# Moving a router fold to the layer transition, and another element order in the output copies, in a two-layer attention and mixture-of-experts kernel

## Chip, cores and metric

The kernel runs on one core of a Trainium2 chip. The metric is the device time of one execution in microseconds. The engines work side by side and meet only at semaphores: TensorE (PE in the rows; its weight loads are PEld), VectorE (DVE), ScalarE (ACT), GpSimd (POOL) and SyncE (SP), which here only starts DMAs. Each engine runs its own instructions in the order in which they are written.

## The reference

x has 4 x 24 x 16 tokens of 256 channels (1536 tokens). Twice, with other weights:

```python
x = x + attention(_ln_c(x))                  # 16 heads of 16
t = tokens(x)
t = t + moe(_ln_t(t))                        # 8 experts, top 2

# attention: q and k are means over the 16 pixels, so scores are 24 x 24 per head and batch;
# v keeps the pixels
out = softmax(q k^T / 4) v                   # reshaped back to (B, N, P, C)
y = out @ W_proj + b_proj
# moe, layer 0: softmax(x @ gate_w + gate_b), top 2, silu(x @ w1 + b1) @ w2 + b2, weighted
# moe, layer 1: top 2 of x @ router_w, softmax of the two, (a * silu(g)) @ W2 + b2, weighted
```

Both norms subtract the mean and divide by the deviation, without weights. All is float32.

## The kernel before

One core holds x in `xres`, 12 tiles of 128 tokens. Per layer the stages follow each other: norm, transposes, attention, projection with the residual, second norm and router logits, a table that sorts token and expert pairs into blocks of 128 rows, and a loop of MoE blocks, which takes most of the time. Nobody plans the order: it is written out by hand, one instruction stream per engine.

**The router fold.** The logits of the second norm are linear in x, so the kernel adds E = 8 columns to the attention's products rather than transposing the normalised x again. For that it needs, per layer, (1) the column-centred router weights, kept in columns 3C to 3C+E of `wqkv` (`centre()`, L940, on VectorE, after column sums on TensorE, L1330), (2) `b_route` = centred weights times the projection bias, two small products (L949), (3) the projection weights transposed on TensorE (L1406) and copied to `wprojT` (L1023), (4) their product with the centred weights (L1414) and the sum of `b_route` over channels (L1417), all in bank 5, and (5) two small copies of the results to `wproj` and `b_logit` (L1028, L1030). Semaphore `fold` counts 7 steps per layer, `fold_mm` 3. Before the change both layers do (3) to (5) within the attention: TensorE between `scores(3)` and `attn_transpose(0)`, VectorE between the softmax steps.

**Attention.** TensorE makes values for two pixels at a time (`values(j)`, L1360) in three banks that ScalarE empties (L731), the scores (L1371), the transposes of the probabilities (L1379), attention times values (L1434), then 8 groups of four transposes (L1445). ScalarE (even groups, L789) and VectorE (odd groups, L1046) copy these from PSUM to `outT`; the projection (L1458) waits for all eight. VectorE adds the projection to `xres` (L1073) and takes statistics (L916). Part of the logits goes through DRAM and back (`x_logits`) and is scaled on VectorE (L1063, L1064).

**Weight rounding.** Expert weights are split in a high and a low part. For the first three experts there are 12 pieces: ScalarE rounds a piece (`first_high`, L686), GpSimd subtracts (L611). Both share the time of the attention; `first_high(a, b)` calls stand between ScalarE's other steps. Piece 10 of GpSimd waits until VectorE has done the x_logits sums (`HELD_SPLIT`). All three experts go through one raw buffer, so a piece's DMA waits for an earlier piece's subtraction.

**The transition.** At the end of layer 0's blocks the rows of the last two blocks are not scattered but added on chip: TensorE multiplies them by one-hot rows (`last_rows(j, n)`, L1589) for six pairs of tiles, VectorE adds pair j to `xres` (L963), takes statistics (L916, L922), ScalarE the square root (`deviations`, L696), VectorE the reciprocal and `less_mean` (L933), and the normalised tiles (ScalarE L702, VectorE L937) are transposed (L1344) and copied (L707). VectorE sums pixels from the same banks (`xm`, L988), from which come queries and keys (L1392). `keep_busy` (L1324) are filler products without result.

Of the kernel before, what the change touches and what calls it, by code (L numbers as in the profile page):

```python
# [46 lines left out]
EARLY_PAIRS = (1, 2)  # L47
HELD_SPLIT = 10
# [99 lines left out]
def metaformer(nc, x, conv_w, ffn_w, out):  # L148

    with ExitStack() as ctx:  # L150
# [526 lines left out]
        def _(act):  # L677
# [10 lines left out]
            for L in range(2):  # L688
# [73 lines left out]
                values_out(5)  # L762
                attn_out(0)
                attn_out(1)
                if L == 0:
                    first_high(5, 6)
# [7 lines left out]
                first_high(*((6, 8), (8, 9))[L])  # L774
                for j in range(0, 8, 2):
                    act.wait_ge(s.av_mm, j + 1)
                    if j == 0:
                        act.wait_ge(s.aT_mm, HGROUPS)
                    nc.scalar.copy(o_sb[:, :, 2 * HD * j:2 * HD * (j + 1)].rearrange("p q (h d) -> p h q d", h=2),
                                   bank[j % 4][0:BN, :].rearrange("p (h q d) -> p h q d", h=2, q=PIX)  # L780
                                   ).then_inc(s.o_act, 1)
                    if j < 4:
                        first_high(8 + L + j // 2, 9 + L + j // 2)
# [3 lines left out]
                for j in range(0, 8, 2):  # L787
                    act.wait_ge(s.oT_mm, j + 1)
                    nc.scalar.copy(outT[:, j // 4, :, 4 * (j % 4):4 * (j % 4) + 4].rearrange("p n q -> p q n"),  # L789
                                   bank[4 + j % 4][:, 0:4 * BN].rearrange("p (q n) -> p q n", q=4)).then_inc(s.o_act, 1)  # L790

                first_high(10 + L, 12)
# [102 lines left out]
                if L == 0:  # L895
                    high_pieces(1, 0, PIECES)
                    nc.scalar.activation(table_out[:, 4:5], all_ones[:, 0:1], ACT.Sqrt)


        @block.vector  # L900
        def _(dve):
# [5 lines left out]
            for L in range(2):  # L907
# [32 lines left out]
                def centre():  # L940
                    dve.wait_ge(fold_mm, FOLD_MM * L + 1)
                    dve.wait_ge(s.route_in, 48 if L == 0 else 32)
                    centred = wqkv[:, :, 3 * C:3 * C + E]
                    nc.vector.scalar_tensor_tensor(out=centred, in0=bank[5][:, 0:E].unsqueeze(1).to_broadcast([P, KC, E]),
                                                   scalar=-1.0 / C, in1=wroute[:, :, :], op0=ALU.mult, op1=ALU.add
                                                   ).then_inc(fold, 1)
                    dve.wait_ge(fold, FOLD * L + 1)
                    for k in range(KC):
                        nc.vector.tensor_scalar(b_route[:, k, :], centred[:, k, :], b_col[:, k:k + 1], None, ALU.mult  # L949
                                                ).then_inc(fold, 1)  # L950
# [40 lines left out]

                dve.wait_ge(s.qk_mm, 1)
# [34 lines left out]
                dve.wait_ge(fold_mm, FOLD_MM * L + 3)  # L1027
                nc.vector.tensor_copy(wproj[:, :, C:C + E], bank[5][:, 0:KC * E].rearrange("p (k e) -> p k e", k=KC)  # L1028
                                      ).then_inc(fold, 1)
                nc.vector.tensor_copy(b_logit[:, :], bank[5][:, KC * E:KC * E + E]).then_inc(fold, 1)  # L1030
# [13 lines left out]
                for j in range(1, 8, 2):  # L1044
                    dve.wait_ge(s.oT_mm, j + 1)
                    nc.vector.tensor_copy(outT[:, j // 4, :, 4 * (j % 4):4 * (j % 4) + 4].rearrange("p n q -> p q n"),  # L1046
                                          bank[4 + j % 4][:, 0:4 * BN].rearrange("p (q n) -> p q n", q=4)
                                          ).then_inc(s.o_dve, 1)
# [264 lines left out]
        def _(pe):  # L1313
# [18 lines left out]

            pe.wait_ge(busy_ready, 1)
# [3 lines left out]
            for L in range(2):  # L1337
# [46 lines left out]
                pe.wait_ge(fold, FOLD * L + 1)  # L1384
# [19 lines left out]
                for kd in range(KC):  # L1404
                    for k in range(KC):
                        mm = pe.transpose(bank[5][:, (KC * kd + k) * P:(KC * kd + k + 1) * P],  # L1406
                                          wproj[:, k, kd * P:(kd + 1) * P], ident[:, :])
                mm.then_inc(fold_mm, 1)
                values(4)
                values(5)  # L1410
                pe.wait_ge(fold, FOLD * L + 4)
                for k in range(KC):
                    for kd in range(KC):
                        pe.matmul(bank[5][:, k * E:(k + 1) * E], wprojT[:, kd, k * P:(k + 1) * P],  # L1414
                                  wqkv[:, kd, 3 * C:3 * C + E], start=(kd == 0), stop=(kd == KC - 1))
                for k in range(KC):
                    mm = pe.matmul(bank[5][:, KC * E:KC * E + E], all_ones[:, :], b_route[:, k, :],  # L1417
                                   start=(k == 0), stop=(k == KC - 1))
                mm.then_inc(fold_mm, 1)
# [183 lines left out]
                if L == 0:  # L1603
# [37 lines left out]
```

## Time and profile before

| | |
|---|---|
| three runs, us | 573.47, 575.12, 576.9 (median 575.12) |
| span of the profiled execution | 569.2 us; its own time outside the span is not listed |
| PE busy | 527.7 us, 93% |
| PE weight loads | 468.0 us, 82% |
| VectorE busy | 342.1 us, 60% |
| ScalarE busy | 347.2 us, 61% |
| GpSimd busy | 254.5 us, 45% |
| chain that ended last | PE 70%, VectorE 12%, issue 5%, DMA 4%, ScalarE 4% |
| mean granted TensorE clock | 0.984 |

The span runs from the first to the last instruction of one profiled execution; the runs' times also hold what lies around it. "Busy" is a sum over the whole span and says nothing of a single stage; the chain of waits tells which engine a stage hangs on. Layer 0's attention lies at about 14 to 64 us, its blocks at 83 to 278, the transition at 278 to 300, layer 1's attention to 345, its blocks from 366 on.

### The profile page before, as it was taken

The numbers are of one execution on the slowest core, as the hardware profiler recorded it, in microseconds if no ns is written. First come the engines' busy times: TensorE is split into PE (matmuls) and PEld (weight loads), VectorE is DVE, ScalarE is ACT, GpSimd is POOL, SyncE is SP. The second block draws the span as 40 slices with busy tenths as digits, with TensorE's granted clock in tenths as the row PEclk, the third lists the DMA queues.
The fourth block names the chain that finished last, engine by engine and source line by source line (L and its number), as shares of the span: only waits on it lengthen the run. The fifth ranks groups of instructions, "written<-read, shape, count | busy, mean of one in ns | idle before, by whom it ended". The sixth has DMA issues, their size and how long they took to land.

```text
span 569.2 us, 15318 instructions
## 1 busy us (share of the span) xinstructions
PE 527.7 (93%) x3512; PEld 468.0 (82%) x3513; DVE 342.1 (60%) x791; ACT 347.2 (61%) x676; POOL 254.5 (45%) x278
## 2 busy tenths in 40 slices
PE   7999969999999999999979999699999999999982
PEld 3887538889999999998858874499999999999981
DVE  6448874555533555554794578755677676757441
ACT  6776545666655666666457745555777676676530
POOL 4649033443544455553515360424444455545422
PEclk9999989999999999999989999899999999999997
DMA  8636825876432543226432238354365555212110
GB/s 277 184 108 154 291 89 145 270 183 175 119 56 39 144 120 83 35 37 178 134 132 86 69 108 268 117 196 116 98 180 133 138 150 160 47 35 41 32 19 10
DMA packets 49037, 70.54 MB, mean 124 GB/s; under 512 B 9182, under 2 KB 40560, under 8 KB 49008
## 3 DMA queue, kind: packets, MB, share of 16 engines
q1 hardware_dynamic: 35216, 56.41, 31.4%
q0 software_dynamic: 10464, 13.58, 13.4%
q10 hardware_dynamic: 3328, 0.20, 0.4%
q8 instruction: 14, 0.23, 0.2%
q14 instruction: 15, 0.12, 0.1%
HBM read 57.55 MB, written 13.47 MB: 125 GB/s over the span
## 4 chain that ended last, share of the span: by engine, by line
PE 70%; DVE 12%; issue 5%; DMA 4%; ACT 4%; DVEq 2%; ACTq 1%; POOLq 0%; POOL 0%
PE banks L1316 16%; PE banks L1318 16%; PE banks L1317 16%; PE banks L1532 6%; PE banks L1360 5%; PE banks L1434 2%; DVE stats L916 2%; PE banks L1497 2%; PE banks L1371 1%; DMA mid_dram<-region_b,scol 1%; ACT onehot_blk L812 1%; DMA expert_io<-xn_dram,gcol 1%; PE banks L1324 1%; DVEq L1197 1%; DVE xres L1073 1%
## 5 line engine op out<-in xcount | busy, mean ns | idle before, releaser
L1316 PE MATMUL banks<-w_hi,xT_hi 128*128 x336 | 119.3, 355 | 4.0 <-DVE xT_lo L1188 2.6
L1318 PE MATMUL banks<-w_hi,xT_lo 128*128 x336 | 114.9, 342 | 0.0
L1317 PE MATMUL banks<-w_lo,xT_hi 128*128 x336 | 114.3, 340 | 0.0
L1316 PE MATMUL banks<-w_hi,hT_hi 128*128 x364 | 107.9, 296 | 3.8 <-DVE hT_lo L1263 3.8
L1317 PE MATMUL banks<-w_lo,hT_hi 128*128 x364 | 102.8, 282 | 0.0
L1318 PE MATMUL banks<-w_hi,hT_lo 128*128 x364 | 102.8, 282 | 0.0
L638 POOL DMA_INDIRECT mid_dram<-region_b,scol x26 | 50.7, 1948 | 74.8 <-DMA mid_dram<-region_b,scol 22.3
L611 POOL TENSOR_TENSOR w_lo<-raw,w_hi 128x1024 fp32r<-128x1024 f32 (+2 forms) x24 | 58.9, 2468 | 52.9 <-ACT w_hi L686 42.3
L836 ACT COPY banks<-seed_rows 128x672 f32 (+1 forms) x84 | 69.0, 822 | 19.8 <-DVE h_sb L1280 10.0
L638 POOL DMA_INDIRECT out_dram<-region_b,scol x26 | 45.7, 1757 | 72.1 <-DVE region_b L1298 19.7
L1316 PEld LDWEIGHTS banks<-w_hi,hT_hi 128*128 128x128 f32 x364 | 69.3, 190 | 7.2 <-issue 6.3
L627 POOL DMA_INDIRECT expert_io<-xn_dram,gcol x52 | 53.0, 1020 | 41.5 <-POOL gcol L623 41.5
L1263 DVE TENSOR_TENSOR hT_lo<-banks,hT_hi 128x512 fp32r<-128x512 f32 (+1 forms) x112 | 63.5, 587 | 12.2 <-issue 5.4
L857 ACT CAST hT_hi<-banks 128x512 fp32r<-128x512 f32 (+1 forms) x112 | 55.2, 535 | 25.4 <-PE banks L1532 24.2
L1316 PEld LDWEIGHTS banks<-w_hi,xT_hi 128*128 128x128 f32 x336 | 63.2, 188 | 8.3 <-issue 4.9
L870 ACT ACTIVATE h_sb<-banks 128x512 f32<-128x512 f32 x56 | 33.5, 599 | 59.0 <-PE banks L1318 57.2
L1317 PEld LDWEIGHTS banks<-w_lo,hT_hi 128*128 128x128 f32 x364 | 69.5, 191 | 0.0
L1318 PEld LDWEIGHTS banks<-w_hi,hT_lo 128*128 128x128 f32 x364 | 69.4, 191 | 0.0
L1318 PEld LDWEIGHTS banks<-w_hi,xT_lo 128*128 128x128 f32 x336 | 63.0, 188 | 4.7
L1317 PEld LDWEIGHTS banks<-w_lo,xT_hi 128*128 128x128 f32 x336 | 63.4, 189 | 3.4
L1197 DVE TENSOR_TENSOR w_lo<-raw,w_hi x40 | 48.4, 1209 | 16.5 <-issue 15.7
L1532 PE MATMUL banks<-ident,h_sb 128*128 128x128 f32 (+1 forms) x392 | 52.0, 272 | 0.0
(206 smaller groups left out, 898.2 us busy)
## 6 DMA issues: line engine op xcount, KB each, us to landing
raw<-in_L_ffn_w_dram SPq DMA_DIRECT2D x32, 512.0 KB, 4.0
raw<-in_L_ffn_W_dram SPq DMA_DIRECT2D x16, 672.0 KB, 4.0
seed_rows<-in_L_ffn_b_dram SPq DMA_DIRECT2D x8, 672.0 KB, 4.5
seed_rows<-in_L_ffn_b_dram SPq DMA_DIRECT2D x8, 512.0 KB, 3.9
xn_dram<-raw SPq DMA_DIRECT2D x6, 512.0 KB, 3.2
raw<-in_L_ffn_W_dram SPq DMA_DIRECT2D x8, 384.0 KB, 3.4
raw<-in_L_ffn_W_dram SPq DMA_DIRECT2D x8, 256.0 KB
wqkv<-in_L_conv_W_qkv_dram SPq DMA_DIRECT2D x2, 768.0 KB, 5.8
```

What stands on the lines that cost most here:

```text
L611: pool.tensor_tensor(w_lo[:, e, at], raw[:, 0, at], w_hi[:, e, at].bitcast(F32), ALU.subtract).then_inc(s.pool_split, 1)
L627: pool.indirect_dma_start(out=xg[:, half * C:(half + 1) * C], out_offset=None, in_=xn_dram, in_offset=bass.IndirectOffsetOnAxis(ap=rows, a ...
L638: pool.indirect_dma_start(out=acc, out_offset=bass.IndirectOffsetOnAxis(ap=scol[:, n:n + 1], axis=0), in_=rows, in_offset=None, bounds_che ...
L836: nc.scalar.copy(banks[:, chunks, 0:f.chunk], seed_row(L, e % SEED_ROWS)[:, 0:f.wide] .rearrange("p (c n) -> p c n", c=f.chunks)[:, chunks ...
L857: nc.scalar.copy(hT_hi[:, part, :], bank[4 + j][:, 0:(part.stop - part.start) * P] .rearrange("p (k s) -> p k s", s=P)).then_inc(s.hT_hi, 1)
L870: nc.scalar.activation(h_sb[:, f.chunk * j:f.chunk * (j + 1)], bank[j][:, 0:f.chunk], ACT.Silu).then_inc(s.h, 1)
L1197: less = nc.vector.tensor_tensor(low, raw[rows, (q // PIECES) % 2, at], w_hi[rows, slot, at].bitcast(F32), ALU.subtract)
L1263: nc.vector.tensor_tensor(hT_lo[:, part, :], bank[4 + j][:, 0:(part.stop - part.start) * P] .rearrange("p (k s) -> p k s", s=P), hT_hi[:, ...
L1316: pe.matmul(out, hi, w_high, start=first, stop=False, skip_group_check=onto)
L1317: pe.matmul(out, hi, w_low, start=False, stop=False, skip_group_check=onto)
L1318: return pe.matmul(out, lo, w_high, start=False, stop=last, skip_group_check=onto)
L1532: mm = pe.transpose(bank[4 + j][0:rows, o:o + P], tile, ident[:, :])
```

## The change

Layer 1's steps (2) to (5) move to the transition. TensorE does them between `last_rows` of pairs 1 and 2 (transposes) and of pairs 3 and 4 (products); ScalarE, behind its last rounding of layer 0, does the `b_route` scalings and the copies that VectorE did. Layer 0 keeps its fold in the attention; its `b_route` products move on VectorE behind the xm sums. The copies to `outT` go through the same elements in another order: before, the inner loop ran over n (PSUM in order, writes 16 words apart), now over q (4 neighbours written, PSUM read BN = 96 words apart). In layer 0 pieces 5, 6, ... of the rounding on ScalarE stand one place earlier.

```diff
+FOLD_PAIRS = (1, 3)
 # ScalarE, attention
+                if L == 0:
+                    first_high(5, 6)
                 attn_out(0)
                 attn_out(1)
                 if L == 0:
-                    first_high(5, 6)
+                    first_high(6, 7)
...
-                first_high(*((6, 8), (8, 9))[L])
+                first_high(*((7, 9), (8, 9))[L])
...
-                        first_high(8 + L + j // 2, 9 + L + j // 2)
+                        first_high(9 + j // 2, 10 + j // 2)
...
-                    nc.scalar.copy(outT[:, j // 4, :, 4 * (j % 4):4 * (j % 4) + 4].rearrange("p n q -> p q n"),
-                                   bank[4 + j % 4][:, 0:4 * BN].rearrange("p (q n) -> p q n", q=4)).then_inc(s.o_act, 1)
-
-                first_high(10 + L, 12)
+                    nc.scalar.copy(outT[:, j // 4, :, 4 * (j % 4):4 * (j % 4) + 4],
+                                   bank[4 + j % 4][:, 0:4 * BN].rearrange("p (q n) -> p n q", q=4)).then_inc(s.o_act, 1)
+
+                first_high(11, 12)
 # ScalarE, end of layer 0
                     nc.scalar.activation(table_out[:, 4:5], all_ones[:, 0:1], ACT.Sqrt)
+                    act.wait_ge(fold, FOLD + 1)
+                    for k in range(KC):
+                        nc.scalar.activation(b_route[:, k, :], wqkv[:, k, 3 * C:3 * C + E], ACT.Identity,
+                                             scale=b_col[:, k:k + 1]).then_inc(fold, 1)
+                    act.wait_ge(fold_mm, FOLD_MM + 2)
+                    nc.scalar.copy(wprojT[:, :, :], bank[5][:, :].rearrange("p (k c) -> p k c", k=KC)).then_inc(fold, 1)
+                    act.wait_ge(fold_mm, FOLD_MM + 3)
+                    nc.scalar.copy(wproj[:, :, C:C + E], bank[5][:, 0:KC * E].rearrange("p (k e) -> p k e", k=KC)
+                                   ).then_inc(fold, 1)
+                    nc.scalar.copy(b_logit[:, :], bank[5][:, KC * E:KC * E + E]).then_inc(fold, 1)
 # VectorE: the b_route products leave centre() ...
+                def bias_logits():
                     dve.wait_ge(fold, FOLD * L + 1)
                     for k in range(KC):
...
 # ... and stand behind the xm sums, in layer 0 alone
+                if L == 0:
+                    bias_logits()
                 dve.wait_ge(s.qk_mm, 1)
...
-                    if g == HGROUPS - 1:
-                        dve.wait_ge(fold_mm, FOLD_MM * L + 2)
+                    if L == 0 and g == HGROUPS - 1:
+                        dve.wait_ge(fold_mm, 2)
...
+                dve.wait_ge(fold, FOLD * L + 6)
                 dve.wait_ge(s.v, PIX)
 # VectorE's copies to outT change as ScalarE's do
...
 # TensorE, attention
-                pe.wait_ge(fold, FOLD * L + 1)
+                pe.wait_ge(fold, FOLD * L + (1, 6)[L])
                 values(0)
...
+                if L == 0:
+                    wproj_transpose()
                 values(4)
                 values(5)
+                if L == 0:
+                    fold_router(L)
 # TensorE, end of layer 0
                         last_rows(j, 1).then_inc(rows_mm, 1)
+                        if j == FOLD_PAIRS[0]:
+                            pe.wait_ge(lay[1].conv_in, 48)
+                            pe.wait_ge(fold, FOLD + 1)
+                            wproj_transpose()
+                        if j == FOLD_PAIRS[1]:
+                            fold_router(1)
                     keep_busy(BUSY_LAYER, 6)
```

`wproj_transpose()` and `fold_router(of)` hold the instructions of L1406 and of L1414 and L1417, unchanged; `fold_router` begins with a wait for `wprojT`, `fold` at 4 of its layer.

## Rows read from the trace of the kernel before

**Rows 1.** Chain of waits, layer 1's attention: start us, us, engine and line.

```profile
312.06 0.44 PE banks L1406 x4
...
316.11 0.79 PE banks L1414 x8
316.90 0.45 PE banks L1417 x4
```

**Rows 2.** Chain of waits, transition and layer 1's output.

```profile
287.49 0.68 DVE xres L963
...
294.67 2.84 PE banks L1344 x12
...
298.16 2.10 PE banks L1360 x8
...
330.04 1.32 PE banks L1445 x16
...
333.85 3.81 PE banks L1458 x16
```

**Rows 3.** Timeline of the transition: start, us, engine, line, operation, [idle before, releaser].

```profile
277.52 7.20 POOL L611 TENSOR_TENSOR w_lo<-raw,w_hi 128x1056 fp32r<-128x1056 f32 x3 [6.72 <-DVE raw L1242]
...
279.40 8.88 PE L1589 MATMUL banks<-raw 128*128 128x256 f32 x40
...
279.80 2.56 DVE L949 TENSOR_SCALAR b_route<-wqkv,b_col 128x8 f32<-128x8 f32 x2
...
285.56 0.30 ACT L696 ACTIVATE std<-mean_var,eps_col 128x4 f32<-128x4 f32 x1 [6.00 <-DVE mean_var L922]
285.67 1.88 POOL L611 TENSOR_TENSOR w_lo<-raw,w_hi 128x800 fp32r<-128x800 f32 x1
...
286.99 0.57 DVE L933 SCALAR_TENSOR_TENSOR less_mean<-mean_var,rstd 128x4 f32<-128x4 f32 x1
...
290.23 1.24 PE L1324 MATMUL banks<-busy_in 128*128 128x512 bf16 x5
...
294.88 3.10 DVE L988 TENSOR_REDUCE xm<-banks 128x32 f32<-128x512 f32 x5
```

**Rows 4.** TensorE by stretches: bounds, length, busy (records), granted clock, DMA share, GB/s.

```profile
67.30:68.70 1.40, 0.00 (x1) 1.00 0.59 205
291.50:293.65 2.15, 0.00 (x0) 1.00 0.00 0
295.00:298.00 3.00, 2.49 (x12) 0.50 0.02 5
```

**Rows 5.** Views of single lines: copies, ns min/median/max, first and last start.

```profile
L789 ACT COPY region_b<-banks x8: 801/830/857, 46.9 to 332.6; 128x384 f32<-128x384 f32 x8
...
L1046 DVE COPY region_b<-banks x8: 802/815/841, 47.2 to 332.9; 128x384 f32<-128x384 f32 x8
...
L743 ACT COPY region_d<-banks x8: 475/476/479, 34.2 to 320.6; 96x384 f32<-96x384 f32 x8
```

**Rows 6.** Groups of instructions by form, VectorE, 64 to 80 us: count, busy, mean ns.

```profile
L1102 DVE TENSOR_TENSOR pick<-expert_m,i_top 128x96 f32<-128x96 f32 x2 | 0.6, 324 | 0.1
L1100 DVE TENSOR_TENSOR expert_io<-expert_io,expert_m 128x96 f32<-128x96 f32 x2 | 0.5, 257 | 0.1
```

**Rows 7.** Timeline of layer 0.

```profile
10.79 0.37 DVE L949 TENSOR_SCALAR b_route<-wqkv,b_col 128x8 f32<-128x8 f32 x2
...
18.55 0.36 DVE L994 COPY region_d<-banks 128x192 f32<-128x192 f32 x1 [2.12 <-PE banks L1392]
...
34.24 0.85 ACT L743 COPY region_d<-banks 96x384 f32<-96x384 f32 x2 [1.18 <-PE banks L1379]
...
41.15 11.06 POOL L611 TENSOR_TENSOR w_lo<-raw,w_hi 128x1024 fp32r<-128x1024 f32 x4 [2.67 <-ACT w_hi L686]
...
50.15 2.17 DVE L1063 TENSOR_TENSOR x_logits<-x_logits,std 128x96 f32<-128x96 f32 x1
50.34 10.92 PE L1458 MATMUL banks<-wproj,region_b 128*128 128x264 f32 x48 [0.95 <-ACT region_b L789]
```

More of the change, by code:

```diff
@@ L946, in centre @@
                                                    ).then_inc(fold, 1)
+                def bias_logits():
                     dve.wait_ge(fold, FOLD * L + 1)
                     for k in range(KC):
-                        nc.vector.tensor_scalar(b_route[:, k, :], centred[:, k, :], b_col[:, k:k + 1], None, ALU.mult
-                                                ).then_inc(fold, 1)
+                        nc.vector.tensor_scalar(b_route[:, k, :], wqkv[:, k, 3 * C:3 * C + E], b_col[:, k:k + 1], None,
+                                                ALU.mult).then_inc(fold, 1)
                 if L == 1:
@@ L1026, in _ @@
                         sm_back(g - 1)
[L1027 to L1030, printed above, removed]
+                if L == 0:
+                    dve.wait_ge(fold_mm, 3)
+                    nc.vector.tensor_copy(wproj[:, :, C:C + E], bank[5][:, 0:KC * E].rearrange("p (k e) -> p k e", k=KC)
+                                          ).then_inc(fold, 1)
+                    nc.vector.tensor_copy(b_logit[:, :], bank[5][:, KC * E:KC * E + E]).then_inc(fold, 1)
+                dve.wait_ge(fold, FOLD * L + 6)
                 dve.wait_ge(s.v, PIX)
@@ L1045, in _ @@
                     dve.wait_ge(s.oT_mm, j + 1)
-                    nc.vector.tensor_copy(outT[:, j // 4, :, 4 * (j % 4):4 * (j % 4) + 4].rearrange("p n q -> p q n"),
-                                          bank[4 + j % 4][:, 0:4 * BN].rearrange("p (q n) -> p q n", q=4)
+                    nc.vector.tensor_copy(outT[:, j // 4, :, 4 * (j % 4):4 * (j % 4) + 4],
+                                          bank[4 + j % 4][:, 0:4 * BN].rearrange("p (q n) -> p n q", q=4)
                                           ).then_inc(s.o_dve, 1)
@@ L1331, in column_sums, with wproj_transpose, fold_router @@
                 mm.then_inc(fold_mm, 1)
+            def wproj_transpose():
+                for kd in range(KC):
+                    for k in range(KC):
+                        mm = pe.transpose(bank[5][:, (KC * kd + k) * P:(KC * kd + k + 1) * P],
+                                          wproj[:, k, kd * P:(kd + 1) * P], ident[:, :])
+                mm.then_inc(fold_mm, 1)
+            def fold_router(of):
+                pe.wait_ge(fold, FOLD * of + 4)
+                for k in range(KC):
+                    for kd in range(KC):
+                        pe.matmul(bank[5][:, k * E:(k + 1) * E], wprojT[:, kd, k * P:(k + 1) * P],
+                                  wqkv[:, kd, 3 * C:3 * C + E], start=(kd == 0), stop=(kd == KC - 1))
+                for k in range(KC):
+                    mm = pe.matmul(bank[5][:, KC * E:KC * E + E], all_ones[:, :], b_route[:, k, :],
+                                   start=(k == 0), stop=(k == KC - 1))
+                mm.then_inc(fold_mm, 1)
             pe.wait_ge(busy_ready, 1)
@@ L1403, in _ @@
                 scores(3)
[L1404 to L1408, printed above, removed]
+                if L == 0:
+                    wproj_transpose()
                 values(4)
                 values(5)
[L1411 to L1419, printed above, removed]
+                if L == 0:
+                    fold_router(L)
                 attn_transpose(0)
```

## The prediction

> **What bounds the kernel now.** I read the chain of waits first, around the places that the diff touches, then the timeline of the same microseconds for the engines that the chain doesn't name. In layer 1's attention the chain runs on TensorE without a break, and layer 1's fold stands in it as three entries: four transposes of the projection weights, eight products of the fold, four of the bias: 0.44, 0.79 and 0.45 us [rows 1]. Between the layers the chain is VectorE's: adding the last rows to x and taking statistics. The timeline shows a hole there: in front of the first addition the two small b_route products took 2.56 us, and ended when the second of GpSimd's three subtractions (7.20 us for three, 2.40 each, so at 282.3) ended; two such products in layer 0 took 0.37 [rows 3, 7]. Behind the statistics come twelve transposes that took 2.84 us and the first values, at half clock until about 298 [rows 2, 4]. In layer 0 the chain is TensorE's again up to the output copies.
>
> **Layer 1's fold leaves the attention.** TensorE loses 0.44 + 0.79 + 0.45 = 1.68 us [rows 1]. What could be late instead: the copies of values by ScalarE follow TensorE, so they move with it. The softmax on VectorE loses the wprojT copy, so it is not later. I count all of it: -1.68.
>
> **The fold arrives at the transition.** TensorE's 40 records of the row products run from 279.40 at 0.22 us each, four to a product set [rows 3]. The order becomes: two sets (to 281.1), the transposes (281.6), four sets (285.1), the fold (1.24, to 286.3), four sets (289.8), then the filler. The row products of pairs 4 and 5 are ready at 288.1 and 289.8; VectorE takes pair 3 at 287.49 [rows 2] and needs 1.8 us for a pair, so it asks at 289.3 and 291.1: hidden.
> VectorE without its b_route products could add pair 0 at 280.3, not 282.27. But it gets nothing for these 2 us. Its next wait is for the first deviation, a square root that ScalarE took at 285.56 after 6.00 us of idleness [rows 3]. ScalarE now has five instructions in front of it, in order: two b_route scalings (279.8, hidden), the wprojT copy (281.6, hidden), and the two small copies that wait for the fold's end at 286.3. With 0.2 us for each small copy (an estimate: its 128x4 square root took 0.30 [rows 3]) the square root starts near 286.75 and not 285.56, and VectorE has it at 287.1 instead of 286.8. Then the shift of less_mean, which took 0.57 us because it too ended with GpSimd's subtraction (285.67 + 1.88 = 287.55) [rows 3], ends at 287.6 as before. So pair 3 starts at 287.5 as before. The transposed copies behind it come late: TensorE's filler and first transposes slide by 1.68, to 291.5 for the second group, ScalarE is free of both copies at 292.3, normalises one tile, and meets the third deviation at 292.9 against 292.8. The fold's arrival costs 0 to 0.3; I take 0.05.
>
> **The clock.** Before, the second filler ended at 291.47 [rows 3], TensorE did nothing for 2.15 us, and in the stretch 295 to 298 the granted clock was 0.50, which is 1.2 of 2.4 GHz [rows 4]. With the fold in front, the filler ends near 292.6 and the idle stretch shrinks to some 1.1 us. Layer 0's idle stretch of 1.40 us left the clock at 1.00 [rows 4]. At full clock the twelve transposes take 1.42, not 2.84 [rows 2], and the values start 1.2 to 1.4 earlier than 298.16. Behind them the query and key products wait for six reductions that take 3.10 us for five from 294.88 [rows 3], so to 298.6, or 298.8 with the fold's lag; they began at 298.16 + 2.10 = 300.26 [rows 2]. The gain lies between 0 (it falls anyway, or a normal run of the kernel before does not have this dip) and 1.4; I take 1.2.
> The Trainium skill (TensorE: Matmul & The Clock Gate, "What's actually happening") says that the clock is one of two levels, set by how busy the array has been; the rows here agree with two levels, and by it the gain is there in some executions only.
>
> **The output copies.** Each of eight copies per layer, half on each engine, writes 384 elements to places 64 bytes apart and takes 0.83 us on ScalarE and 0.815 on VectorE; a ScalarE copy of 384 elements written in order takes 0.476 [rows 5]. On VectorE the same form of 96 elements takes 324 ns when its writes are spread and 257 when not, 0.70 ns an element [rows 6]; 384 x 0.70 = 0.27 us, which leaves 0.55. The new order writes four neighbours at a time but reads PSUM 384 bytes apart, and no row shows such a read. Bounds: 0.55 (free), 0.82 (a spread PSUM read costs what a spread write did: no gain), and 1.07 (it costs twice that). I take 0.60, nearest to the contiguous row. The copies then follow TensorE's transposes: in layer 1 TensorE's eight groups of four take 0.33 us each from 330.04 (16 in 1.32) and so deliver the last at 332.7; VectorE's last copy ends at 333.3 and the projection starts at 333.4, where it started at 333.85 [rows 2]. That is 0.42 for each layer, -0.84 in all; at 0.82 us it is 0, at 1.07 it is +1.0 for each layer (four copies on VectorE, each 0.26 longer).
> The Trainium skill (SBUF — State Buffer, "Door 1: The DMA port swizzle") gives SBUF lines of 16 bytes and PSUM lines of 8, with a penalty for leaving a line: the new writes fill their lines, the new reads leave one each time. No row here shows the PSUM side; by it the copies gain little or nothing, my first rival.
>
> **Layer 0's rounding, one piece earlier.** ScalarE sat idle 1.18 us before the first attention copy at 34.24 [rows 7]; piece 5 (1.05 us) fits in there. GpSimd then starts it 1.9 us earlier and its run of four subtractions (11.06 us to 52.2) becomes three. VectorE's product on x_logits, 2.17 us because it ended only with that run, falls to what such a product takes undisturbed, 0.26 [rows 6, 7]. Worth by itself: it and its 0.26 us successor ended at 52.6; TensorE's first pair was ready at 50.34 + 10.92 x 8/48 = 52.16 [rows 7], VectorE catches up 0.2 a pair, and the end is TensorE's last pair. So 0, but with the copies 0.42 earlier it is the cover that they need. A piece lands later than ScalarE asks for it at 0 to 0.5 us' cost; I take 0.
>
> **Layer 0's b_route behind the reductions.** It took 0.37 in front of VectorE's normalising [rows 7]; the deviation that follows was ready 0.1 before, so -0.1. At its new place VectorE waits 2.12 us for query and key products [rows 7]. If it meets GpSimd as at the transition (2.56 us [rows 3]) the key copy is at most 0.4 late; TensorE has two rounds of values to do first. Hidden.
>
> **The sum.** -1.68 + 0.05 - 1.2 - 0.84 - 0.1 = -3.8 us. The profiled span is 569.2; which of the runs it is, is not shown, so its own time is taken as the median, 575.12, with 5.9 us around the span. 575.1 - 3.8 = 571.3.
>
> **Rivals.** (a) The PSUM reads eat the copies' gain: 575.1 - 3.8 + 0.84 = 572.2. For it: the lone price above is for SBUF. Against: no row that reads PSUM so. (b) The clock gives nothing, since it falls after all, or since the other runs before never had the dip: 575.1 - 2.6 = 572.5. For it: the runs lie 3.4 us apart. (c) ScalarE's ordered wait bites. VectorE and the square root stand behind the fold's end; if the fold's products wait for the wprojT copy, or the small copies take 0.5 rather than 0.2, pair 3 is 1.0 to 1.5 late and everything behind it: 571.3 + 1.25 = 572.6. Against: 3.5 us lie between the transposes and the fold. (d) Slower: the spread PSUM reads cost so much that the copies pass all other gains. The others give 2.9; four copies a layer lie one behind the other on VectorE, eight in all, so the point is a copy of 0.815 + 2.9/8 = 1.18 us. At 1.35 us it is 8 x 0.535 - 2.9 = +1.4, 576.5. Against: twice the known penalty gives only 1.07. That the change does nothing is excluded by the fold alone, 1.68 us of uninterrupted TensorE.
>
> **Numbers.** Forecast 0.42, (a) 0.20, (b) 0.20, (c) 0.10, (d) 0.08. A measurement of this kernel can tell some 0.5%, 2.9 us, so faster means under 572.2. Of the forecast nearly all falls there, of (a) nearly half and of (b) and (c) a third: 0.56. Slower takes (d) and nothing else: 0.07. Range 569.0 to 574.6: the upper end takes in (a) to (c) with a median of before that was 1.5 low; the lower one 1.4 for the clock, free copies and 1.5 of spread.
>
> **What would show it.** In the changed trace: layer 1 from the last score to the last value shorter by 1.7 with L1406, L1414 and L1417's successors near 281 and 285; the first square root of layer 1 behind two small copies near 286.7; pair 3 still near 287.5; clock 1.00 at 295 to 298; output copies near 0.6 (or 0.8: rival a); x_logits' product 0.26 in layer 0. The prediction is wrong if the square root comes after 287.5, or if the copies take over 1.1.

## The result and the profile after

| | before | after |
|---|---|---|
| median of 20 runs each, us | 575.19 (570.9 to 580.12) | 570.15 (568.05 to 578.36) |
| ratio, 95% interval | | 0.9938 [0.9915, 0.9961] |
| profiled execution: span, its own time, us | 569.2, about 571 | 568.1, 569.87 |
| mean granted clock in it | 0.984 | 0.981 |

The change made the kernel 0.62% faster, 3.6 us by the ratio. The ratio leaves out a few disturbed runs, which the two medians, 5.0 us apart, do not. Repeated beside the kernel before (`after_again` below) it was 0.9942.

The spans of the two profiled executions differ by only 1.1 us, so a reader of the two pages alone would see a third of the effect. The stages show why. This table is worked out from the two timelines of TensorE: each column is the time between the starts of two marker products (s: span start; qk: first query and key product; av: first attention times values; pr: first projection product; tab: first product of the block table; ffn: first expert product; cs: column sums at the transition; 0 and 1 are layers).

```
        s>qk0 qk0>av0 av0>pr0 pr0>tab0 tab0>ffn0 ffn0>cs cs>qk1 qk1>av1 av1>pr1 pr1>tab1 tab1>ffn1 ffn1>end
before  16.49  22.89   10.96   26.44     6.82    195.44  21.06   22.78   10.97   25.81     7.01    202.53
after   16.69  22.89   10.57   26.46     8.25    195.04  19.88   21.10   10.57   25.81     7.86    202.98
```

Four stages got shorter, 1.18 us at the transition, 1.68 in layer 1's attention and 0.39 and 0.40 in front of the projections: 3.65 us. Two stages that the change doesn't touch, from the table to the first expert product, were longer by 1.43 and 0.85 in this one execution, because the clock was low for longer (`list_filler` below). In all nine profiled executions of the changed kernel and its variants with this filler the two together took 14.56 to 16.45 us, against 13.83 in the only one of the kernel before; one page can't show whether the change has a part in that. The chain of waits of the changed kernel, layer 1 from the transition to its projection (start us, us, what):

```profile
282.24 0.44 PE banks L1355 x4
282.67 3.46 PE banks L1616 x16
286.13 0.79 PE banks L1363 x8
286.92 0.45 PE banks L1366 x4
287.37 3.56 PE banks L1616 x16
290.92 0.86 PE banks L1343 x4
...
292.26 1.07 ACT region_b L708 x2
...
295.54 0.67 PE banks L1381 x4
...
297.84 2.10 PE banks L1397 x8
...
328.11 2.32 PE banks L1472 x28
330.45 0.49 ACT region_b L792
330.94 0.51 issue
331.45 3.81 PE banks L1485 x16
```

The three entries of the fold, 0.44, 0.79 and 0.45 us as in [rows 1], now stand among the row products (L1616, L1589 before) and no longer in the attention. There they are again on the chain: it no longer goes through VectorE as in [rows 2] but through TensorE, then ScalarE's copies. In the timeline of the transition, the same microseconds on the other engines:

```profile
280.65 0.49 ACT L903 ACTIVATE b_route<-wqkv,b_col 128x8 f32<-128x8 f32 x2 [0.25 <-DVE wqkv L957]
281.51 0.69 DVE L978 TENSOR_TENSOR xres<-xres,banks 128x512 f32<-128x512 f32 x1 [0.89 <-PE banks L1616]
...
287.40 0.17 ACT L908 COPY wproj<-banks 128x16 f32<-128x16 f32 x1 [4.11 <-PE banks L1366]
287.47 0.17 ACT L910 COPY b_logit<-banks 128x8 f32<-128x8 f32 x1
287.53 0.31 ACT L697 ACTIVATE std<-mean_var,eps_col 128x4 f32<-128x4 f32 x1
...
288.34 0.68 DVE L978 TENSOR_TENSOR xres<-xres,banks 128x512 f32<-128x512 f32 x1
...
292.49 1.24 PE L1343 MATMUL banks<-busy_in 128*128 128x512 bf16 x5
...
294.55 0.66 PE L1381 MATMUL banks<-ident,region_a 128*128 128x128 f32 x4 [0.81 <-ACT region_a L703]
```

The square root sits behind the two small copies of the fold, which take 0.17 us each. The column sums start at 279.90 here and at 279.04 before (sums of the table's columns), so 0.86 us is to be taken off for a comparison: the square root is at 286.67 on the old scale, and pair 3's addition at 287.48, where it was in [rows 2]. The idle time of TensorE behind the filler is 0.81 us.

Stretches of TensorE (bounds, length, busy, granted clock, DMA share, GB/s), the first three as in [rows 4]; there the third stood at 0.50:

```profile
67.30:68.70 1.40, 0.16 (x3) 1.00 0.61 205
291.50:293.65 2.15, 2.15 (x15) 1.00 0.23 74
295.00:298.00 3.00, 1.89 (x15) 1.00 0.02 5
```

The output copies, as in [rows 5], by line:

```profile
L792 ACT COPY region_b<-banks x8: 478/478/478, 47.2 to 330.5; 128x384 f32<-128x384 f32 x8
```

```profile
L1065 DVE COPY region_b<-banks x8: 557/558/559, 47.5 to 330.8; 128x384 f32<-128x384 f32 x8
```

The copies also free their banks sooner. Layer 0's attention times values and the transposes behind it, in the kernel before and then in the changed one:

```profile
39.38 7.16 PE L1434 MATMUL banks<-raw,region_d 96*96 96x256 f32 x32 [0.46 <-ACT raw L731]
46.37 3.02 PE L1445 MATMUL banks<-ident,region_a 96*128 96x96 f32 x32
```

```profile
39.58 7.22 PE L1461 MATMUL banks<-raw,region_d 96*96 96x256 f32 x32 [0.46 <-ACT raw L732]
46.64 2.80 PE L1472 MATMUL banks<-ident,region_a 96*128 96x96 f32 x32
```

The last four groups of transposes write to the banks of the first four and wait for their copies; the eight now take 2.80 us and not 3.02. The products ahead of them take 0.06 us longer, which nothing in the change asks for.

And layer 0's timeline around the projection, answering to [rows 7]:

```profile
41.42 8.71 POOL L612 TENSOR_TENSOR w_lo<-raw,w_hi 128x1024 fp32r<-128x1024 f32 x3 [2.45 <-ACT w_hi L687]
```

```profile
50.49 0.26 DVE L1082 TENSOR_TENSOR x_logits<-x_logits,std 128x96 f32<-128x96 f32 x1 [0.45 <-DMA x_logits<-x_logits_dram]
50.79 0.26 DVE L1083 TENSOR_TENSOR x_logits<-x_logits,b_logit 128x96 f32<-128x96 f32 x1
52.27 0.69 DVE L1092 TENSOR_TENSOR xres<-xres,banks 128x512 f32<-128x512 f32 x1 [1.23 <-PE banks L1485]
```

### The profile page after: what moved, and what is told of

Read it like the earlier page. It is cut to its first block, busy times and chain, and to the rows that moved or that the text cites. A ratio compares the mean times of both kernels' runs of the same rounds, so it can differ in the third digit from the quotient of the medians.

```text
span 568.1 us, 15321 instructions
## 1 busy us (share of the span) xinstructions
PE 527.5 (93%) x3512; PEld 467.3 (82%) x3513; DVE 334.6 (59%) x786; ACT 345.6 (61%) x681; POOL 252.6 (44%) x278
## 4 chain that ended last, share of the span: by engine, by line
PE 70%; DVE 8%; DMA 7%; issue 5%; ACT 4%; DVEq 2%; POOL 1%; ACTq 1%; POOLq 1%; SPq 0%
PE banks L1335 15%; PE banks L1337 14%; PE banks L1336 14%; PE banks L1559 5%; PE banks L1397 5%; DMA out_dram<-region_b,scol 5%; PE banks L1461 3%; PE banks L1524 2%; PE banks L1616 2%; PE banks L1343 2%; DVE stats L929 1%; PE banks L1485 1%; PE banks L1408 1%; ACT onehot_blk L815 1%; DMA expert_io<-xn_dram,gcol 1%
```

## The experiments

Twelve runs: eleven other kernels and, as `after_again`, the changed one once more. Those in one group of the table ran beside the same runs of the kernel before. Stage columns are as above, tab is the sum of both layers' tab>ffn.

```
                 median us (runs)  ratio to before            span   av0>pr0 pr0>tab0 cs>qk1 qk1>av1  tab
before (page)         -                                       569.2   10.96   26.44   21.06   22.78  13.83
after (page)     570.15 (20)  0.9938 [0.9915, 0.9961]         568.1   10.57   26.46   19.88   21.10  16.11

fold_back        573.46 (12)  0.9973 [0.9934, 1.0013]         571.7   10.49   26.48   22.36   23.05  15.83
filler_for_fold  573.09 (12)  0.9994 [0.9955, 1.0032]         567.9   10.49   26.47   19.89   22.79  15.45
old_copies       570.48 (12)  0.9931 [0.9895, 0.9967]         572.4   11.03   26.49   19.88   21.10  16.07
fold_as_filler   568.92 (12)  0.9902 [0.9864, 0.9940]         568.7   10.56   26.48   18.54   21.11  15.02

root_first       569.73 (12)  0.9952 [0.9919, 0.9984]         568.9   10.56   26.45   19.88   21.10  15.24
old_rounding     569.54 (10)  0.9938 [0.9897, 0.9978]         572.0   10.56   26.81   19.88   21.10  14.60
list_filler      569.56 (12)  0.9937 [0.9913, 0.9961]         565.1   10.56   26.45   19.88   21.10  13.39
best2            569.40 (12)  0.9911 [0.9874, 0.9947]         570.5   10.56   26.45   20.40   21.35  13.20

best3            568.26 (9)   0.9912 [0.9879, 0.9945]         565.0   10.56   26.50   17.93   21.10  13.21
after_again      571.07 (12)  0.9942 [0.9905, 0.9979]         568.5   10.56   26.48   19.88   21.10  16.45
runs_of_two      568.07 (1)        -                          566.3   10.56   26.50   19.88   21.11  14.56
before_list      571.81 (1)        -                          569.8   10.97   26.48   21.07   22.78  13.22
```

A ratio's interval is 0.5 to 0.8% wide, 2.6 to 4.7 us, so it can't size an effect of 1 us. The stages, which repeat to 0.01 or 0.02 us in undisturbed stretches, can. The verdicts below go by the stages and use the ratios as a check.

**fold_back.** The whole move of layer 1's fold undone, the rest of the change kept.

```diff
-                        if j == FOLD_PAIRS[0]: ... wproj_transpose()
-                        if j == FOLD_PAIRS[1]: fold_router(1)
...
-                if L == 0:
-                    wproj_transpose()
+                wproj_transpose()
```

> The changed kernel with layer 1's fold back in its attention (TensorE and VectorE), all other parts kept. My theory (the fold's 1.68 us were uncovered TensorE time there, and at the transition it hides behind VectorE's chain): query/key products of layer 1 to attention times values goes from 20.9 back to 22.6 us. The transition, from the column sums to the query/key products, was 19.9 us with the change and 21.1 before; in this run it is 19.8 to 20.0 where the granted clock stays at 1.00 over the transposes and 21.1 where it falls. Against the changed kernel in all: +1.7 to +2.9 us. Rival (the gain at the transition is VectorE's, which lost its blocked b_route products, not the clock's): the transition is 21.1 or more whatever the clock.

Layer 1's attention went to 23.05 (22.78 before) and the transition to 22.36, as VectorE, stretches and TensorE's timeline show:

```profile
280.21 2.56 DVE L954 TENSOR_SCALAR b_route<-wqkv,b_col 128x8 f32<-128x8 f32 x2
```

```profile
294.09 0.66 PE L1370 MATMUL banks<-ident,region_a 128*128 128x128 f32 x4 [2.22 <-ACT region_a L703]
```

```profile
295.00:298.00 3.00, 2.42 (x12) 0.59 0.03 5
```

TensorE idles 2.22 us in front of the third group of transposes, and the clock is at 0.50 from 296 to 302 and back at 1.00 by 303, past the start of the attention at 301.8. The two gains of the move are both gone. The expectation had 21.1 for a transition in which the clock falls; it took 1.3 us more, since the clock here stayed low for longer than in the kernel before, where it was back at 1.00 from 298. So a fall has no fixed price.

**filler_for_fold.** As fold_back, but eight filler products stand at the transition where the fold's products stood.

```diff
+                        if j == FOLD_PAIRS[0]:
+                            keep_busy(2, 6)
+                        if j == FOLD_PAIRS[1]:
+                            keep_busy(6, 6)
```

> As fold_back, but with eight filler products (1.7 us) on TensorE at the two places at which the changed kernel has the fold. Only the filler's time is in the fold's place, no work of the fold. Clock theory: the transition is 19.7 to 20.0 us with the clock at 1.00 over the transposes, as in the changed kernel, and the attention is 22.6 us. Rival (it is the work moved off VectorE that shortens the transition): 21 us or more even at a clock of 1.00. Third possibility: the transition is under 19.6, since ScalarE does not wait for the fold here; VectorE still has its blocked b_route products, so I expect at most 0.2 of that.

VectorE's blocked products are there, as long as before, and yet the transition is as short as in the changed kernel, 19.89:

```profile
279.48 2.57 DVE L954 TENSOR_SCALAR b_route<-wqkv,b_col 128x8 f32<-128x8 f32 x2
```

```profile
293.38 0.66 PE L1370 MATMUL banks<-ident,region_a 128*128 128x128 f32 x4 [0.88 <-ACT region_a L703]
```

```profile
295.00:298.00 3.00, 2.22 (x15) 1.00 0.02 5
```

So the 1.18 us of the transition are the clock's alone. Filler that pushes the later filler 1.7 us nearer to the late transposes brings them as well as the fold does; that VectorE lost its wait on GpSimd brings nothing. The 1.68 us of the attention are the fold's. The totals are too coarse to confirm it: fold_back and filler_for_fold ran side by side, and their ratios, 0.9973 and 0.9994, do not show the 2.5 us by which the transitions of the two profiled executions differ.

That one profiled execution can catch a fall by chance is answered by the others. In all eight with fold or filler in that place and the rest of the transition's TensorE order as in the changed kernel (after, after_again, filler_for_fold, old_copies, root_first, old_rounding, list_filler, runs_of_two) the clock stayed at 1.00 and the stage took 19.88 or 19.89; in all three without it (before, before_list, fold_back) it fell to 0.50.

**old_copies and runs_of_two.** The copies in the old order; and in an order that writes pairs, `"p n (a b) -> p a n b"` with a = b = 2.

```diff
-  outT[:, j // 4, :, 4 * (j % 4):4 * (j % 4) + 4]
+  outT[:, j // 4, :, 4 * (j % 4):4 * (j % 4) + 4].rearrange("p n q -> p q n")
```

> The changed kernel with the output copies in the old element order (PSUM read in order, writes 64 bytes apart). Theory: copies take 0.83 and 0.815 us again instead of 0.478 and 0.558, the way from attention times values to the projection is 10.97 instead of 10.57 us in each layer, +0.8 us in all. Rival (the projection is held by something else, as the x_logits transfer): under +0.2 us in all though the copies are longer.

> The eight output copies of a layer on each engine write pairs of neighbouring elements (8 bytes) instead of single ones 64 bytes apart (the old copies) or runs of 4 (the new ones), and read pairs of rows of the PSUM bank. Theory (the cost is per separate run that is written, not per element): half-way costs, VectorE's copy about 0.64 us (0.56 with long runs, 0.815 with single elements) and ScalarE's about 0.60 (0.48 and 0.83). Rival (any 4-byte stride on the read or write side costs the same as full spread): 0.8 us and above on both. Second rival (a pair is already as good as a long run): 0.56 and 0.48.

The two copy lines of old_copies, then of runs_of_two (each a view of its own):

```profile
L792 ACT COPY region_b<-banks x8: 799/829/847, 50.2 to 334.9; 128x384 f32<-128x384 f32 x8
```

```profile
L1065 DVE COPY region_b<-banks x8: 803/810/843, 50.5 to 335.3; 128x384 f32<-128x384 f32 x8
```

```profile
L792 ACT COPY region_b<-banks x8: 481/492/509, 47.1 to 329.9; 128x384 f32<-128x384 f32 x8
```

```profile
L1065 DVE COPY region_b<-banks x8: 557/558/559, 47.5 to 330.2; 128x384 f32<-128x384 f32 x8
```

The new order is worth 0.46 and 0.47 us in the two layers' stages, and the same when both kernels have layer 1's fold in the attention: 10.96 and 10.97 in before, 10.49 and 10.50 in fold_back. Against the page of before it shows as 0.39 and 0.40, because every kernel with the fold moved is 0.07 us longer in this stage: its products of attention times values take 7.22 us and not 7.16, in both layers. No run explains those 0.07. Of the 0.47, 0.22 come from transposes that no longer wait for a bank (2.80 against 3.02 us) and the rest, 0.25, from the last copy. Pairs cost what runs of four cost, so the theory of a price per separate run is refuted and the second rival holds: 8 bytes in a row are enough. The Trainium skill (SBUF — State Buffer, "Door 1: The DMA port swizzle") asks for at least two hits in each 16-byte SBUF line, and this agrees: on VectorE and ScalarE one hit cost 815 and 830 ns, two 558 and 492, four 558 and 478. The penalty that the same section gives for leaving an 8-byte PSUM line, which it states for matmuls, does not show for these copies, which read each PSUM element from another line.

**old_rounding.** Layer 0's pieces back in their old places.

```diff
-                if L == 0:
-                    first_high(5, 6)
                 attn_out(0)
                 attn_out(1)
+                if L == 0:
+                    first_high(5, 6)
```

> The changed kernel with layer 0's rounding pieces at their places of before. Theory: VectorE's x_logits product again waits for GpSimd (2.2 us instead of 0.26) and the first addition of the projection starts at the start of the projection + 2.5 instead of + 2.12, but VectorE catches up: projection to the first table product stays at 26.45 us, within 0.05. Rival (the earlier piece is what frees VectorE on the chain's path): 26.45 + 0.4 to 0.8.

```profile
51.05 1.81 DVE L1080 TENSOR_TENSOR x_logits<-x_logits,std 128x96 f32<-128x96 f32 x1 [0.71 <-DMA x_logits<-x_logits_dram]
52.89 0.26 DVE L1081 TENSOR_TENSOR x_logits<-x_logits,b_logit 128x96 f32<-128x96 f32 x1
53.19 0.69 DVE L1090 TENSOR_TENSOR xres<-xres,banks 128x512 f32<-128x512 f32 x1
```

```profile
50.44 10.92 PE L1483 MATMUL banks<-wproj,region_b 128*128 128x264 f32 x48 [0.70 <-ACT region_b L790]
```

The product runs until GpSimd's run of four (41.72 + 11.03 = 52.75) is over. The first addition comes 2.75 us behind the first projection product, against 52.27 - 50.15 = 2.12 in the changed kernel. Of these 0.63 us VectorE makes up 0.24 behind the first pair and 0.03 over the four after it, for from then on it is hardly idle in either kernel (4.99 us busy of 5.20 in both), and the stage from the projection to the table is 0.36 longer: just under the rival's 0.4 to 0.8 and not the theory's nothing. With the copies of before it was hidden (26.44); with the faster ones it is not.

**root_first.** In the changed kernel the square root of pairs 0 and 1 waits on ScalarE behind the fold's small copies. Here it stands ahead of them.

```diff
                 deviations(0, 0)
+                if L == 1:
+                    ... the two small copies of the fold
                 normalise(range(0, 4))
```

> The changed kernel, with ScalarE's two small copies of the fold's result moved from in front of layer 1's first square root to directly behind it; TensorE's order is untouched. Theory (ScalarE's order, not only the fold's place on TensorE, holds the chain by 2.9 us at the first square root): square root 2.9 us earlier, pair 3 added 1.8 us earlier, then pairs 4 and 5 wait for TensorE's row products, which the fold delays, so of 1.8 some 0.9 to 1.1 us arrive: transition 18.8 to 19.0 instead of 19.88 us. Rival (only the fold's place on TensorE counts, as the row products of pairs 4 and 5 are late): transition 19.6 to 19.9.

```profile
287.60 0.69 DVE L979 TENSOR_TENSOR xres<-xres,banks 128x512 f32<-128x512 f32 x1
...
295.33 0.18 DVE L941 RECIPROCAL rstd<-std 128x4 f32<-128x4 f32 x1 [1.13 <-ACT std L697]
```

```profile
293.54 1.07 ACT L708 COPY region_b<-banks 128x512 f32<-128x512 f32 x2 [2.46 <-PE banks L1382]
...
295.00 0.29 ACT L697 ACTIVATE std<-mean_var,eps_col 128x4 f32<-128x4 f32 x1
```

Its column sums start at 281.2. Pair 3 is added 6.4 us behind them and not 8.4; the third square root, 13.8 us behind them, is where it was (293.72 - 279.90). ScalarE stands idle 2.46 us for TensorE's transposes, which follow row products, fold and filler. Two chains of equal length meet there; shortening VectorE's alone gives nothing, and the stage stays at 19.88 where the theory had 18.8 to 19.0.

**fold_as_filler.** The second chain shortened too: the fold's products replace the filler behind the fourth pair of transposes, and the small copies stand last.

```diff
                     if j == 1:
-                        keep_busy(BUSY_CHUNK, 6)
+                        if L == 0:
+                            keep_busy(BUSY_CHUNK, 6)
+                        else:
+                            fold_router(1)
```

> A new place: the transposes stay behind pair 1, but the fold's products replace the filler behind layer 1's first two groups of transposes, and ScalarE makes the two small copies behind its last normalised tile. Theory (in the changed kernel ScalarE's first square root waits 2.9 us behind the fold's end, and VectorE's additions of pairs 3 to 5 then come late): square root near 284.6 on the changed kernel's time scale instead of 287.5, pair 3 added at 286.5 instead of 288.3, pair 5 at 290.0 instead of 291.8, transition 1.5 to 1.9 us shorter: 18.0 to 18.4. Rival (GpSimd's subtractions hold VectorE's less_mean until 288.4 whatever ScalarE does): pair 3 still at 288.3 and the transition 19.9.

The stage fell to 18.54, by 1.34 us, a little less than the theory's 18.0 to 18.4. ScalarE's idle time before the copies fell from the 2.46 of root_first to 2.13, and its third square root came 12.48 us behind the column sums and not 13.82, the same 1.34 earlier.

**best2.** The four filler products ahead of the transposes dropped too (`BUSY_LAYER` 0), and the table stages' filler doubled.

> fold_as_filler with the four filler products in front of layer 1's transposes left out and with list_filler's 34. Theory: the first transposes start 0.9 us earlier, so ScalarE reaches the third square root 0.6 us earlier: transition 17.8 to 18.0 us instead of 18.54 (fold_as_filler) and 19.88 (the changed kernel); with the list's filler the total is 2.5 to 5 us under the changed kernel. Rival: without the four the clock falls over the transposes (0.50), and the transition is 18.9 or more.

```profile
294.55 0.66 PE L1382 MATMUL banks<-ident,region_a 128*128 128x128 f32 x4 [0.86 <-ACT region_a L703]
```

```profile
295.00:298.00 3.00, 2.65 (x14) 0.66 0.02 6
```

The rival was right for this execution: the clock went to 0.50 at 296, and the stage took 20.40. The idle time in front of the transposes, 0.86 us, is about that of the changed kernel (0.81), where the clock held. An idle time alone doesn't tell whether it falls. One profiled execution doesn't tell how often it does either: its own time was 572.27, and the kernel's other runs go down to 565.00, lower than any of the other kernels'.

**best3.** As best2, with three filler products behind the fold.

```diff
                         else:
                             fold_router(1)
+                            keep_busy(3, 6)
```

> The fold's nine products stand where TensorE's filler stood, behind the fourth pair's transposes, with three filler products (0.2 us each) behind them; the four filler products ahead of the transposes are gone, and the table stage has 34 filler products instead of 16. Theory (the filler's work is wanted, only its place was wrong): column sums to layer 1's first q/k product 17.4 to 18.2 us, at clock 1.00 throughout, against 19.9 in the changed kernel, 18.5 with the fold as filler and all fillers kept, and 20.4 without the four fillers; total 566.5 to 568.5 us. Rival (the clock falls because the busy stretch ahead of the third pair of transposes ends 0.9 us too soon, whatever stands behind the fourth): 0.50 appears again between 294 and 303, the transition is 20 us or more, total as the changed kernel, 569 to 570.5.

```profile
291.57 0.66 PE L1382 MATMUL banks<-ident,region_a 128*128 128x128 f32 x4 [0.24 <-ACT region_a L703]
```

```profile
295.00:298.00 3.00, 3.00 (x19) 1.00 0.00 0
```

The stage is 17.93 us, within the theory's 17.4 to 18.2, 1.95 less than in the changed kernel, at full clock. With 568.26 against 571.07 of the changed kernel in the same comparison this is the best transition of the study. The totals don't single it out: the ratios of fold_as_filler, best2 and best3, 0.9902, 0.9911 and 0.9912, can't be told apart, and their intervals overlap the changed kernel's.

**list_filler and before_list.** One number changed, `BUSY_LIST` 16 to 34, in the changed kernel and in the kernel before.

> The changed kernel with 34 instead of 16 filler products on TensorE before the table products of both layers (3.9 us more, inside its 4.36 us of idleness). Theory (the idle stretch drops the clock to 0.50 in every run, for a length that differs from run to run, and most of the spread of the times is from that): clock 1.00 from 72 to 90 and from 350 to 370, first table product to first expert product 6.0 to 6.8 us in both layers instead of 6.8 to 8.3, total 1 to 3 us under the changed kernel, and a narrower spread. Rival (that stretch is paced by the gather's DMA and not by TensorE): the clock stays up, but the stretch is 6.8 and the total falls under 0.5 us. Other rival: the filler ends too late and delays the table products, +0.2 to +0.5 in each layer.

> The kernel before with 34 filler products instead of 16 in the table stages, the edit that held the clock at 1.00 there in the changed kernel (span 565.1 us). Theory (the two changes are independent): table stage to first product 6.7 us in both layers, span 565.1 plus the 3.7 that the stages differ by = 568.8 us or so, transition at 21.1. Rival (the clock's fall at the transition hangs on what happened before): the transition comes out at 19.9 or at 22 and the difference is another one.

Stretches around the gather of the first rows, in the changed kernel and in list_filler:

```profile
75.00:83.00 8.00, 6.39 (x40) 0.57 0.15 42
355.00:363.00 8.00, 5.74 (x38) 0.57 0.23 79
```

```profile
75.00:83.00 8.00, 6.35 (x50) 1.00 0.17 51
355.00:363.00 8.00, 5.54 (x47) 1.00 0.15 41
```

The page of before has 0.79 in both stretches. The table stage has a filler that is too short, and how long the clock stays down behind it differs between executions; at full clock it is 6.7 us in both layers of list_filler (6.75 and 6.47 in before_list), against 8.25 and 7.86. With the tables quiet in both kernels the spans are 569.8 and 565.1: of the 4.7 us between them 3.68 lie in the four stages (transition 1.19, attention 1.68, 0.41 and 0.40 before the projections) and 1.25 in layer 0's blocks, which no run explains. The expected 568.8 for before_list missed that part. The median of list_filler did not follow its span: ratio 0.9937, the changed kernel's own, where 1 to 3 us less had been expected. The narrower spread did come: its 12 runs lie within 5.2 us, those of the changed kernel within 10.3 (20 runs) and 8.6 (12). Other disturbances, of the load at the start and of the blocks, remain in the timed runs.

**after_again.** The changed kernel unchanged.

> The changed kernel itself once more, beside the kernel before on the same chip. Theory (the stages of the two profiles say it: 1.2 us at the transition, 1.7 in layer 1's attention, 0.4 a layer in the output copies): ratio 0.9935, time 3.6 to 3.8 us below the kernel before. Rival (the medians of the first comparison were flattered by runs with different clock in the table stages): ratio 0.997 or above.

The ratio was 0.9942 [0.9905, 0.9979], 3.3 us: as the theory had it, and the rival's 0.997 is inside the interval, near its end. All stages repeated to 0.02 us except the start (17.57), the tables and the blocks.

## Why the prediction was right, step by step

The total alone would not have decided: 0.9915 to 0.9961 is 4.9 to 2.2 us less, and rivals (a), (b) and (c) with their 2.9, 2.6 and 2.5 us lie in that interval beside the forecast's 3.8. What follows goes by the stages.

- **Fold out of the attention, -1.68.** Measured -1.68 (22.78 to 21.10), and back with fold_back. Right.
- **Fold at the transition, hidden.** The predicted square root (286.75) and pair 3 (287.5) came at 286.67 and 287.48 on the old scale, the third square root at 292.86 for 292.9. Right. That VectorE gains nothing by losing its wait on GpSimd was right too, but the reason given was half of it: ScalarE's order holds the first square root, and behind it TensorE's transposes hold ScalarE to the same microsecond, as root_first shows.
- **Clock, -1.2.** Measured -1.18; filler_for_fold isolates it. The idle time shrank to 0.81 (predicted 1.1), and the first query product came at 298.92 on the old scale (predicted 298.8; it stood at 300.10 before, not at the 300.26 that the text added up). Rival (b) finds nothing for it in the profiled executions: the clock fell there in all three without the moved work and in none of the eight with it. That the size fits is partly luck: the page of before, from which it was read, and before_list had a fall that cost 1.2 us, fold_back one that cost 2.5. How often the clock falls in the runs without a profile, and for how long, is not shown.
- **Output copies, -0.84.** Measured -0.39 and -0.40 by the pages, of which the copies are -0.47 and the unexplained 0.07 goes against them (old_copies, fold_back). The copies took 0.558 and 0.478 and not 0.60: the lower bound (0.55) was the truth. The path was half right: the last copy on VectorE is what the projection waits for (330.8 + 0.56 = 331.4; it starts at 331.45), but 0.22 of each 0.47 came earlier, through transposes that had waited for banks, a wait that the text left out. By its own numbers, 333.85 less 333.4, the gain was 0.45 and not 0.42. Rivals (a) and (d) fall with the first copy line: a spread PSUM read costs nothing here.
- **Layer 0's rounding, 0.** The product did fall to 0.26, and the move is needed as the cover of the faster copies, as the text said. But "VectorE catches up 0.2 a pair" was wrong: it caught up 0.24 behind the first pair and 0.03 in all after that, so the move is worth 0.36, and without it the faster copies would have brought almost nothing in layer 0.
- **b_route in layer 0, -0.1.** Not seen: the first query product starts at 16.69 (16.49 before), and VectorE then waits 0.30 us for the deviation. At its new place the longer of the two products took 1.36 us beside GpSimd, hidden as said. In root_first the two took 4.31 us there, VectorE's copy of the keys came 2.0 us later than in the changed kernel, well over the 0.4 that the text allowed, and still nothing was lost: the attention's first stage took 22.90 us against 22.89.
- **The sum, -3.8.** The stages give -3.65, the ratio -3.6, that is 571.6 from the median of before; the median of the changed kernel was 570.15.
- **Base.** "5.9 us around the span" was wrong. In each of the 227 timed runs whose span is on record the time is the span plus 1.7 to 2.4 us, so the profiled execution of before took about 571 and was among the fastest of its runs (570.9, 571.21), not the median. The sum subtracted from the median was still a good forecast of a median. The likely reason is that the slower runs lose their time where the change does nothing: the profiled executions differ most in the load at the start (16.33 to 19.80 us to the first query product), the tables and layer 0's blocks (194.6 to 200.7 us). No profiled run of the kernel before is a slow one, so this is argued and not shown.

Rival (c), ScalarE's wait behind the fold, did not bite at this size: the wait is there, 4.11 us of idleness ahead of the small copies, but a second chain of equal length hides it, which the text had not seen.

## What to carry to other kernels

Copy out of PSUM in the order that suits the SBUF side: two neighbouring fp32 writes were as good as four, and the strided PSUM read was free. When work that pays for itself elsewhere (here the fold) can stand where filler stands, it pays twice; but each filler product that is taken away or pushed must be looked at for the clock in the stage behind it. Compare kernels by stages between marker instructions where the totals spread more than the effect.

## What the runs showed of the hardware

- These small products on VectorE, with operands in SBUF, lasted until a GpSimd subtraction of 2.4 us ended: 128x8 ones took 2.56 us for two (4.31 in layer 0 of root_first), 128x96 ones 1.81 to 2.17 us, and 0.26 where GpSimd was idle. ScalarE's b_route products beside the same GpSimd run took 0.49 for two. Moving this work to ScalarE removed the coupling.
- Most of the spread between runs goes with TensorE's mean granted clock: over the 20 timed runs of the changed kernel a mean clock lower by 0.01 goes with 5.3 us more (correlation -0.92); over 89 runs of the kernel before, without one of 670 us, the correlation is -0.85.
- The same idle time of 0.8 to 0.9 us before the transposes left the clock at 1.00 in eight profiled executions and was followed by 0.50 in best2, which differed in the work ahead of it; 2.2 us were followed by 0.50 in three of three. What decides between the two is not settled.
